# Gated LoRA feed-forward in seven products: the two y tiles of a block made in one stay instead of two

## What is computed

```python
W = weights[condition]                         # 64 x 64 x 64
y = einsum('bct,bcd->bdt', x, W)               # per batch row
logits = y_flat @ gate_w.T + expert_bias       # 4096 x 4
one_hot = one_hot(argmax(logits), 4)
base = y_flat @ W_up.T                         # 4096 x 1024 x 1024
z = einsum('nh,erh->ner', y_flat, lora_A)      # rank 8, 4 experts
delta = einsum('ner,ehr,ne->nh', z, lora_B, one_hot)
out = x + base + delta
```

## Time and profile before

| | us |
|---|---|
| median of 3 runs | 406.57 (406.15 to 406.83) |
| the profiled execution | 406.41 |
| its span, first to last instruction | 404.6 |
| PE busy in it | 398.1 (98%) |
| PEld busy | 357.3 (88%) |
| DVE busy | 301.7 (75%) |
| ACT busy | 110.2 (27%) |
| POOL busy | 132.4 (33%) |
| granted TensorE clock, mean | 0.999 of full speed |

### The profile page before, as it was taken

How to read it: one execution, slowest core, us unless ns; L and a number is a source line. 1 busy time by engine, 2 the same in 40 slices (tenths; PEclk the granted TensorE clock), 3 DMA queues, 4 the chain that set the end, 5 groups by cost and what they waited for, 6 DMA issues and landing times.

```text
span 404.6 us, 9746 instructions
## 1 busy us (share of the span) xinstructions
PE 398.1 (98%) x3451; PEld 357.3 (88%) x3451; DVE 301.7 (75%) x717; ACT 110.2 (27%) x226; POOL 132.4 (33%) x123
## 2 busy tenths in 40 slices
PE   7999999999999999999999999999999999999997
PEld 7898988979888898888979798898988889798996
DVE  3899668889876858776696766867677766967675
ACT  5896211323114031211213131131311303131310
POOL 1689211628031250505205080221605043050700
PEclk9999999999999999999999999999999999999999
DMA  7910240503214132313125031150322221250102
GB/s 251 358 58 2 83 139 28 190 26 113 79 67 151 39 100 105 132 56 103 54 83 186 28 109 70 40 183 26 110 104 89 99 78 58 104 181 28 54 33 98
DMA packets 20993, 39.39 MB, mean 97 GB/s; under 512 B 7494, under 2 KB 7750, under 8 KB 20970
## 3 DMA queue, kind: packets, MB, share of 16 engines
q1 hardware_dynamic: 17600, 27.40, 18.6%
q10 hardware_dynamic: 3370, 11.69, 9.1%
HBM read 22.30 MB, written 16.78 MB: 97 GB/s over the span
## 4 chain that ended last, share of the span: by engine, by line
PE 96%; DMA 1%; SPq 1%; ACT 1%; issue 0%; DVE 0%
PE bank_y L878 23%; PE bank_x L878 22%; PE bank_b L878 11%; PE bank_c L929 10%; PE y_ps L791 7%; PE bank_c L1083 5%; PE bank_b L1083 4%; PE bank_x L856 2%; DMA cond_pair<-in_L_cond_weights_dram 1%; PE bank_c L878 1%; PE bank_b L884 1%; PE bank_x L884 1%; PE bank_y L884 1%; PE bank_c L884 1%; PE bank_y L856 1%; PE y_ps L1157 1%
## 5 line engine op out<-in xcount | busy, mean ns | idle before, releaser
L878 PE MATMUL bank_y<-w_s,hl_s 128*128 128x292 f32 (+1 forms) x384 | 51.5, 290 | 0.0
L878 PEld LDWEIGHTS bank_y<-w_s,hl_s 128*128 128x128 f32 x384 | 49.2, 188 | 2.5 <-issue 2.5
L878 PE MATMUL bank_x<-w_a,hl_a 128*128 128x256 f32 (+1 forms) x384 | 50.8, 288 | 0.0
L878 PEld LDWEIGHTS bank_x<-w_a,hl_a 128*128 128x128 f32 x384 | 49.5, 188 | 0.3 <-issue 0.2
L878 PE MATMUL bank_b<-w_s,hl_s 128*128 128x512 f32 x192 | 47.7, 397 | 0.1
L878 PE MATMUL bank_y<-w_a,hl_a 128*128 128x292 f32 x360 | 47.7, 288 | 0.0
L878 PEld LDWEIGHTS bank_y<-w_a,hl_a 128*128 128x128 f32 x360 | 46.6, 188 | 0.3
L307 POOL TENSOR_TENSOR s_sum<-a 128x512 f32<-128x512 f32 x9 | 11.9, 1328 | 102.4 <-DVE a L1403 101.9
L878 PE MATMUL bank_x<-w_s,hl_s 128*128 128x292 f32 x336 | 44.6, 289 | 0.0
L929 PE MATMUL bank_c<-w_s,hl_s 128*128 128x512 f32 x168 | 44.4, 409 | 0.0
L307 POOL TENSOR_TENSOR s_sum<-a,a_even 128x512 f32<-128x512 f32 x7 | 9.1, 1297 | 106.1 <-DVE a_even L1403 106.1
(11 more groups left out here) (194 smaller groups left out, 622.0 us busy)
## 6 DMA issues: line engine op xcount, KB each, us to landing
out_dram<-x_sb SPq DMA_DIRECT2D x63, 256.0 KB, 2.0
x_sb<-in_x_dram ACTq DMA_DIRECT2D x22, 512.0 KB, 3.6
x_sb<-in_x_dram SPq DMA_DIRECT2D x10, 512.0 KB, 3.3
w_raw<-in_L_ffn_W_up_dram SPq DMA_DIRECT2D x8, 512.0 KB, 5.7
cond_pair<-in_L_cond_weights_dram SPq DMA_DIRECT2D x64, 16.0 KB, 2.8
out_dram<-x_sb SPq DMA_DIRECT2D x2, 128.0 KB, 1.9
router_sb<-in_L_ffn_lora_A_dram ACTq DMA_DIRECT2D x1, 128.0 KB
lora_b_sb<-in_L_ffn_lora_B_dram SPq DMA_DIRECT2D x1, 128.0 KB, 5.2
```

The source lines that it names most:

```text
L878: mm = pe.matmul(dst, hl[op][:, a, k, :], w[:, b, k, cols], start=(fresh and k == 0 and a + b == 0), stop=(k == KH - 1 and a == 1), skip_g ...
```

## The change

In `one` and in every `even` block both tiles' y is made in one stay, behind p6: tile 0 in `y_ps` as before, tile 1 in `bank_b` and `bank_c`. p7 follows, then the turning of z 0, then p5. Waits go with it: those for tile 1's input and pair, and for `c12_out` and `c22_out` of the block before, now stand ahead of p6's last two matmuls; in `one` the wait for `p4_out` stands ahead of p6; ahead of the turning of z 0 stands a wait for all transposes (`y_summed`). DVE turns the second tile right behind the first, rounds out p7 and the second routing ahead of p5, and in `one` runs `rebuild(0, 1)` behind `after_delta11`. ACT takes `round_a11` and `round_a12` ahead of `move_z` for z 0. The odd blocks are as they were.

```diff
+        Y_FIRST = [y_ps[:, 0, :], y_ps[:, 1, :]]
+        Y_SECOND = [bank_b[:, 0, :], bank_c[:, 0, :]]
...
# ACT, one
-                move_z(q, 1, 0, bank_c[:, 0, :])
                 round_a11(q + 1, True)
                 round_a12(q + 1, True)
+                move_z(q, 1, 0, bank_c[:, 0, :])
                 move_z(q, 1, 1, chains[0][:, 1, :])
...
# ACT, even
+                round_a11(q + 1, True)
+                round_a12(q + 1, True)
                 move_z(q, 0, 0, bank_c[:, 0, :])
-                round_a11(q + 1, True)
...
-                round_a12(q + 1, True)
                 move_z(q, 0, 1, chains[1][:, 1, :])
...
+            def wait_second_y(q, par):
+                pe.wait_ge(x_loaded[2 * par + 1], 8 * (q - par) + 16)
+                pe.wait_ge(pair_loaded[2 * par + 1], 16 * (q - par) + 32)
+                pe.wait_ge(c12_out, q - 1)
+                pe.wait_ge(c22_out, q - 1)
...
# PE, one
                 pe.wait_ge(p1_out, q + 1)
-                multiply("s2", q, chain, False, lambda: wait_y_inputs(q + 1, 0, 0))
+                pe.wait_ge(p4_out, q)
+                multiply("s2", q, chain, False, lambda: (wait_y_inputs(q + 1, 0, 0), wait_second_y(q + 1, 0)))
                 make_y(q + 1, 0, 0)
-                pe.wait_ge(p4_out, q)
+                make_y(q + 1, 0, 1, Y_SECOND)
+                pe.wait_ge(u2_out, q + 1)
+                multiply("s3", q, chain, False)
+                pe.wait_ge(y_summed, 4 * q + 8)
                 turn_z(bank_c[:, 0, 0:P], q, 0)
-                pe.wait_ge(c22_out, q)
                 multiply("s1", q, bank_b, True)
                 delta11_of(q, pair)
-                pe.wait_ge(u2_out, q + 1)
-                multiply("s3", q, chain, False, lambda: wait_y_inputs(q + 1, 0, 1))
-                make_y(q + 1, 0, 1)
                 third_product(q, pair)
...
# PE, even: the same, without p4_out; the wait for c12_out ahead of turn_z goes
...
# DVE, one
                 turn_y(q + 1, 0, 1, a12)
+                turn_y(q + 1, 1, 0, a21, Y_SECOND)
+                turn_y(q + 1, 1, 1, a22_even, Y_SECOND)
+                low_operand(dve, "a11", a11, q + 1)
+                after_p7(q, 1)
+                route(q, 1, 1)
...
                 rebuild(0, 0)
+                after_p5(q, 1)
+                after_delta11(q, 1)
                 rebuild(0, 1)
-                after_p5(q, 1)
-                low_operand(dve, "a11", a11, q + 1)
-                after_delta11(q, 1)
                 rebuild(1, 0)
                 rebuild(1, 1)
                 low_operand(dve, "a12", a12, q + 1)
-                after_p7(q, 1)
-                route(q, 1, 1)
-                turn_y(q + 1, 1, 0, a21)
-                turn_y(q + 1, 1, 1, a22_even)
                 after_delta12(q, 1)
...
# DVE, even
                 turn_y(q + 1, 0, 1, a12)
+                turn_y(q + 1, 1, 0, a21, Y_SECOND)
+                turn_y(q + 1, 1, 1, a22, Y_SECOND)
+                low_operand(dve, "a11", a11, q + 1)
+                after_p7(q, 0)
+                route(q, 0, 1)
+                low_even_a22(g)
                 after_p5(q, 0)
-                low_operand(dve, "a11", a11, q + 1)
                 after_delta11(q, 0)
...
-                low_even_a22(g)
                 low_operand(dve, "a12", a12, q + 1)
-                after_p7(q, 0)
-                route(q, 0, 1)
-                turn_y(q + 1, 1, 0, a21)
-                turn_y(q + 1, 1, 1, a22)
                 after_delta12(q, 0)
```

More of the change, by code:

```diff
@@ L783, in wait_y_inputs, with make_y @@
                 pe.wait_ge(y_summed, 4 * q + 2 * t)
-            def make_y(q, par, t):
+            def wait_second_y(q, par):
[3 more added lines that the diff above has]
+                pe.wait_ge(c22_out, q - 1)
+            def make_y(q, par, t, to=Y_FIRST):
                 for d in range(2):
@@ L790, in make_y @@
                             at = b * D + d * STRIP
-                            mm = pe.matmul(y_ps[j * STRIP:(j + 1) * STRIP, b, d * QUARTER:(d + 1) * QUARTER],
+                            mm = pe.matmul(to[b][j * STRIP:(j + 1) * STRIP, d * QUARTER:(d + 1) * QUARTER],
                                            cond_pair[rows, 2 * par + t, at:at + STRIP],
@@ L1064, in even @@
                 pe.wait_ge(p1_out, q + 1)
-                multiply("s2", q, chain, False, lambda: wait_y_inputs(q + 1, 1, 0))
+                multiply("s2", q, chain, False, lambda: (wait_y_inputs(q + 1, 1, 0), wait_second_y(q + 1, 1)))
                 make_y(q + 1, 1, 0)
-                pe.wait_ge(c12_out, q)
+                make_y(q + 1, 1, 1, Y_SECOND)
+                pe.wait_ge(u2_out, q + 1)
+                multiply("s3", q, chain, False)
+                pe.wait_ge(y_summed, 4 * q + 8)
                 turn_z(bank_c[:, 0, 0:P], q, 0)
-                pe.wait_ge(c22_out, q)
                 multiply("s1", q, bank_b, True)
                 delta11_of(q, pair)
-                pe.wait_ge(u2_out, q + 1)
-                multiply("s3", q, chain, False, lambda: wait_y_inputs(q + 1, 1, 1))
-                make_y(q + 1, 1, 1)
                 third_product(q, pair)
@@ L1394, in _, with turn_y @@
             low_operand(dve, "a22", a22, 1)
-            def turn_y(q, t, h, to):
+            def turn_y(q, t, h, to, source=Y_FIRST):
                 if to is a12:
@@ L1404, in turn_y @@
                         to[:, :].rearrange("p (k b d n) -> p b d k n", k=KH, b=2, d=2)[:, b, :, :, :],
-                        y_ps[:, b, :].rearrange("p (d h k n) -> p h d k n", d=2, h=2, k=KH)[:, h, :, :, :])
+                        source[b].rearrange("p (d h k n) -> p h d k n", d=2, h=2, k=KH)[:, h, :, :, :])
                 turned.then_inc(y_summed, 1)
```

## The result

| | before | changed |
|---|---|---|
| median, us | 406.76 (406.13 to 408.08, 20 runs) | 408.22 (406.57 to 412.52, 20 runs) |
| ratio of the runs | | 1.0039 (95%: 1.0028 to 1.0050) |
| profiled execution | 406.41, span 404.6 | 409.27, span 407.5 |

The account below looks back on a forecast made before the run. TensorE, with a matmul in flight for 98% of the span, was taken to bound the kernel. -2.6 + 1.05 + 1.4 + 2.1 = +1.95 us gave 408.36 profiled, 408.5 as a median; range 406.4 to 410.9.

Parts of the forecast that it names:

- eight stays less: TensorE in `one` and seven even blocks: one stay of y less each, 0.33 us apiece, 2.6 us less (2.3 to 2.9).
- p4 in `one`: Block 1: p6 waits for DVE's drain of p4, the product right ahead of it; 1.05 us more, once (0.9 to 1.2).
- sums of block 2: Later rebuilds on DVE delay POOL's fine sums, so p6 of block 2 starts late; 1.4 us more, once (0.7 to 2.3).
- tile 1's input: Loop's even blocks: the load's wait moves 7.3 us earlier, ahead of p6's last two matmuls; 2.1 us more (0.9 to 4.3).
- What was put at nothing: Waits such as `u2_out`, `y_summed`, `c12_out`, `c22_out` and `c11_out` (0.3 to 0.4 us to spare) cost TensorE nothing.
- (B): Rival, faster: loop loads take 4.3 us or less, TensorE never waits for tile 1, block 2 costs 0.7; 405.7; chance 0.08.
- (C): Rival, about no change: POOL's lateness absorbed in block 2 (407.1), or waits behind tile 1's cost nothing (407.3); chance 0.20.
- (D): Rival, much slower: POOL's sums beside DVE's low parts make `c11_out` late in seven even blocks; 4 to 6 us, 413; chance 0.08.
- (E): Rival: the 0.33 us is the price of a tile, not of a stay, so 2.6 us come back; 411; chance 0.04.

Follow-up runs that it names:

- split again: Kernel with all three mended, plus one small full-shape matmul between the two tiles in block 1 and the seven even blocks: 408.17 us, 3.2 over that kernel.
- the first: Changed kernel with block 1 (`one`) as it was before, only the seven even blocks making both tiles in one stay: 406.23 us, ratio 0.9987 to the kernel before.
- third: Changed kernel with the `p4_out` wait in block 1 moved from ahead of p6 to between the two tiles: 407.12 us, ratio 1.0000 to the kernel before.
- fourth experiment: Changed kernel with block 1's four rebuilds earlier on DVE, two ahead of p6's drain, two behind the eight transposes: 406.79 us, ratio 0.9998 to the kernel before.
- all three mended: Changed kernel with tile 1's waits and block 1's `p4_out` wait between the tiles, and block 1's rebuilds early on DVE: 404.98 us, ratio 0.9956 to the kernel before.

## Why the prediction came out right, step by step

The forecast was 408.5 with the path to it: four terms, three of them costs. Each is now measured, by the trace and by taking it away. (With all lower bounds the prediction's sum gives 406.2, not its 406.3.)

| term | predicted | in the trace | by the experiment |
|---|---|---|---|
| eight stays less | -2.6 | -2.5 (0.31 each, blocks 8 and 10) | split again: +3.2 with its matmuls |
| p4 in `one` | +1.05 | +1.0 | -1.1 |
| sums of block 2 | +1.4 | +1.3 | -1.4 by the medians; -0.76 in block 2 itself, where a pause of 0.5 came |
| tile 1's input | +2.1 | +1.65 | -1.3 |
| sum | +1.95 | +1.5 | |

The third column's pauses are the excess over 20.85 in blocks 4 (0.69), 6 (0.11), 12 (0.45) and 14 (0.40). The last column's differences of medians are good to about 0.5.

**The stays.** The 0.33 was read from three places; 0.31 came. In the new trace z and p5 take 2.87 (I had 2.84), the nine matmuls 2.07 (2.1), p7 behind the stay 3.13 (3.11 before). The Trainium skill's page on array packing (TensorEngine Tiling (Array Packing), Key Properties) says that a change of tiling mode drains TensorE, and that switching tiles within a mode doesn't; the trace agrees, with 1.89 for two tiles in one stay, and 2.38 with one full-shape matmul between them.

**p4 in `one`** and **the sums of block 2** happened as told, down to the order on POOL and DVE: rebuilds complete at 72.4, which is the predicted 71.2 and the 1.2 by which this profile starts later; third sum at 78.23 (77.1 + 1.2 = 78.3), the low part of s2 until 80.06 (78.95 + 1.2 = 80.15). ACT did issue tile 1's load for block 3 late, at 78.19, and it took only 3.3; it was alone on its way, and no pause came of it.

**Tile 1's input** is the step that was mis-sized. I let 0.8 pass between the landing and y's first matmul, with 0.3 of it for the waits behind, whose values are computed in registers. In blocks 4, 6 and 12, where there was a pause, y's first matmul came 0.51, 0.51 and 0.50 after the landing. Of that 0.42 is the two matmuls ahead of y (131.01 to 131.43), so only 0.1 was left for the release and all waits behind, against the 0.45 that I had put there without a row. In block 14, unrolled, the distance was 0.73, with 0.3 ahead of the two matmuls. With no price for the waits behind, the prediction's own figure was 0.9 instead of 2.1. That 1.65 came is in part luck: the loads took 4.6, 4.7, 4.5, 4.4, 5.1 and 4.8 against the earlier trace rows, so that block 14, put at nothing, paid 0.40 and block 12 0.45, and block 4's load was issued 0.35 later against y. In block 4 SP spent 1.1 on the instruction of one store (0.74 before), and the load of tile 1 hangs on the store behind it. The size is a matter of how long each load takes in each run; over the four profiles with the wait in p6's place (the changed kernel's, the first, third and fourth experiment's) it took 4.3 to 5.2 where both loads were in flight.

**What was put at nothing** stayed so. `u2_out`, `y_summed`, `c12_out` and `c22_out` show no wait in any profile. `c11_out` was put 0.3 to 0.4 ahead; 0.67 was measured.

**The rivals.** *(B)* needed loads at or under 4.3: they took 4.4 to 5.1. *(C)* had two ways. POOL's lateness was not absorbed. But its other condition, that the waits behind tile 1's cost nothing, did come true in the loop; its 407.3 did not, since the loads were later than in the trace before. *(D)* had a mechanism that is there: in block 6 DVE's low part of a11, begun ahead of POOL's sum, took 0.65 and the sum 1.65 instead of 1.29, while that of a22, begun behind POOL's next sum, took 0.94, which the Trainium skill (SBUF — State Buffer, Who interferes with whom) describes as taking turns. In block 2 the low part of s2 took 1.21 beside POOL's sum, as it had before the change; what was new there is that both came late. But at `c11_out` 0.67 was left. *(E)* is refuted by the split stay.

What stays open: odd blocks 7, 9 and 11 of the changed kernel take 26.50, 26.47 and 26.49 where those before took 26.40 to 26.41. With block 1 as before and the waits between the tiles, two odd blocks take 26.51, and with all three mended three take 26.51 to 26.54. The extra time stands directly ahead of the next block's p1: from the last matmul to p1's first it is 0.29 to 0.36 there instead of 0.23. In all profiles this happens only ahead of blocks 6, 8, 10 and 12, where TensorE's loop begins a new round, and never in the kernel before. Why only some rounds and some kernels pay it, no run here shows.

## What to carry to other kernels

When work is moved forward, price it at its inputs first: here 2.5 us were won in the sequence and 4.0 lost at three waits. Two of them (p4's drain and tile 1's input) were not needed where they stood, and the third came from rebuilds that had been moved behind other work. Put a wait directly ahead of the work that needs it, where that costs nothing, as it did here between the tiles: ahead of p6's last two matmuls instead of p7's, it turned a transfer with over 7 us to spare (block 6: landed at 174.7, y of tile 1 at 182.71) into a late one. And a helper's work on a slow side engine can be late for the next block even if the engine that waits for it looks idle: look at what starts behind the moved instruction on every queue.

## What the runs showed of the hardware that was not expected

- A wait in the middle of a stay in the small array shape cost nothing, even where its transfer landed 0.4 after the first of 64 matmuls had started: the stay took 1.89 as ever.
- Three waits behind a late one, with values computed in registers, cost at most 0.1 together with the release: 0.51 from landing to y's first matmul in the loop, 0.42 of it two matmuls. In the unrolled blocks, whose values are constants, the same distance was 0.73 (block 14 in three profiles, block 2 in two). The reason of the difference was not looked for.
- One small matmul in the full shape (128 rows, 32 columns) between two tiles of a stay costs 0.5 us with its weight load; a stay less in the sequence gives back 0.31.
